# A transformer block with 32 ranked experts: the late tiles in another order, with their records, transposes and bias products

## The chip, the core and the metric

The kernel runs on one core of a Trainium2 chip. The metric is the device time of one execution in microseconds; before, the median of three runs is 299.98 us (299.43 to 300.33). The profile is one execution of its own, taken by the hardware profiler.

## What is computed

Cut to what matters; `x` has 1024 tokens of 512 numbers, everything is f32.

```python
x = x + ffn0(conv(x, cond_128, weight, c_weight, fside_S_0), w_gate, w_up, w_down)   # grouped conv of 9 taps; silu(gate) * up, down
y = mixed_1x1(x, cond_128, ...)                                                      # per-sample 32x32 kernel and bias
logits = y @ gate_w.T                                                                # 32 experts
w, idx = top_k(logits, 2); w = softmax(w)
combine = zeros((1024, 32)).at[arange(1024)[:, None], idx].add(w)
for e in range(32):
    acc = acc + combine[:, e:e+1] * (y @ expert_w[e].T + expert_b[e])
return x + acc
```

The kernel computes the two chosen experts of each token and no others: it sorts the 2048 pairs of token and expert by expert and multiplies tiles of rows.

## The kernel before

**Stages.** Up to some 125 us TensorE makes the tables of the first feed-forward layer and its first hidden half, and then the rest of that layer; up to about 183 us the last token tiles are routed. From 174 us on the expert stage runs, which is all that the change touches.

**Ranks.** The experts are ranked by how many tokens of the first half of the tokens chose them. Rank r's weights (512 x 512, 1 MB) are read from the place that `order` holds. Every rank has a fixed number of 32-row groups, by the plan at lines 83 to 136; what does not fit goes to a loop at the end that is skipped when nothing is left (line 1600 and below).

**Tiles.** A tile has 128 rows in groups of 32 or 64, each group of one rank: `pairs` gives tiles of two ranks with 64 rows each, `quads` four ranks with 32, `three_and_one` one rank with 96 and one with 32. `GROUPS_OF_TILES` (line 96) lists 21 tiles in the order in which they are worked on. Before it is:

| tiles | ranks |
|---|---|
| 0 to 3 | 0 and 4, 1 and 5, 2 and 6, 3 and 7 |
| 4 | 8, 9, 10, 11 |
| 5 to 8 | 0 and 4, 1 and 5, 2 and 6, 3 and 7 |
| 9 | 0, 1, 2, 3 |
| 10 | 10 and 11 |
| 11 to 14 | 8 and 24, 9 and 25, 12 and 26, 13 and 27 (three groups and one) |
| 15 to 19 | 14 and 19, 15 and 20, 16 and 21, 17 and 22, 18 and 23 |
| 20 | 28, 29, 30, 31 |

Tiles 0 to 4 (below `FIRST` = 5) hold tokens of the first half only. Tiles from 15 (`FIRST_B`) on are multiplied in two halves of 256 output columns, so that the left half of the output can be finished while the right one is computed (`STEPS`, line 133): the left halves of 15 to 19, the right ones of 15 to 17, the left half of 20, the right ones of 18, 19 and 20.

**What each tile does.** SyncE loads its records (`load_recs`, line 535: token, row and weight of each of the 128 rows; tiles of a group share a semaphore). GpSimd gathers the tokens' rows into `yg` (`gather_tile`, 665) and scatters finished rows to `r_tab` (`scatter_step`), one after the other on one queue. TensorE transposes yg (`transposes`, 1462, records at L1459), VectorE copies the result to `xT` (`xt_evac_tile`, 1046, records at L1044), TensorE multiplies with the weights (`product`, 1474, records at L1487; c0 and c1 bound the four chunks of 128 inner rows, two instructions for each group and chunk), and ScalarE evicts it with the row's weight (`evac`, L831). A product raises `r_mm` when it is done, a transposition `xt_mm`. The transposes of tile t+1 stand on TensorE ahead of the product of tile t, or in its middle.

**Weights.** Sixteen buffers of 1 MB hold 32 loads (`load_w`, 523, on SyncE's queue). Loads 0 to 15 fill them: ranks 0 to 11, then 24, 25, 12, 26. Loads 16 to 31 are ranks 13, 27, 14, 19, 15, 20, 16, 21, 17, 22, 18, 23, 28, 29, 30, 31. Each takes the buffer whose last product comes earliest (`SECOND`, 149), and SyncE waits for that product:

```python
                if i >= NA:
                    sp.wait_ge(w_in[b], 16)
                    sp.wait_ge(r_mm, released(b))
```

`released(b)` is one more than the last tile that uses the buffer. Before, loads 16, 17, 18 and 19 wait for products 5, 6, 7 and 8, loads 20 to 23 for product 9, 24 and 25 for 10, 26 and 27 for 11, 28 and 29 for 12, 30 and 31 for 13.

**Beside the tiles.** TensorE also makes the bias products (`bias`, 1429, L1435: the experts' biases by the combine weights, four PSUM banks for each half of the tokens), VectorE adds them (`add_bias`, L1013), and TensorE and VectorE count what is left for the loop at the end (`hist` at L1443, L1591, L1597; VectorE L1148 to L1196).

**The end.** When all left halves are scattered, SyncE reads `r_tab` back (`load_parts`, 591) into weight buffers, VectorE sums (L1211, L1212), and the left half of the output is stored; then the same for the right.

Of the kernel before, what the change touches and what calls it, by code (L numbers as in the profile page):

```python
# [42 lines left out]
P = 128  # L43
# [16 lines left out]
DC = D // P  # L60
# [17 lines left out]
NA, QUAD, PAIR = 16, P // 4, P // 2  # L78
SPLIT, SPLIT_QUAD, NQ = 8, 12, 4
WHOLE, THREE, TWO, ONE = 10, 14, 24, 32  # L80


def pairs(rank, pos, n):
    return [[(PAIR * q, PAIR, rank + i + n * q, pos) for q in range(2)] for i in range(n)]


def quads(rank, pos):
    return [[(QUAD * q, QUAD, rank + q, pos) for q in range(4)]]


def three_and_one(rank, pos, other):
    return [[(QUAD * q, QUAD, rank + i, pos + QUAD * q) for q in range(3)] + [(3 * QUAD, QUAD, other + i, 0)] for i in range(2)]
# [1 line left out]


GROUPS_OF_TILES = (pairs(0, 0, 4), quads(SPLIT, 0),
                   pairs(0, PAIR, 4), quads(0, P), pairs(WHOLE, QUAD, 1),
                   three_and_one(SPLIT, QUAD, TWO), three_and_one(SPLIT_QUAD, 0, TWO + 2),
                   pairs(THREE, 0, 5), quads(TWO + 4, 0))
TILES = [tile for group in GROUPS_OF_TILES for tile in group]  # L100
RECS = tuple(itertools.accumulate(len(group) for group in GROUPS_OF_TILES))
# [104 lines left out]
def build_adaln_ffn(nc, a):  # L206
    ctx = ExitStack()
    with ctx:
# [297 lines left out]
        def _(sp):  # L506
# [54 lines left out]
                store_y(j)  # L561

            sp.wait_ge(recs_out, 2 * NT * 16)
            for g in range(2, 4):
                load_recs(g)
            for r in range(13, NA):
                load_w(r)
            for g in range(4, len(RECS)):
                load_recs(g)
            for r in range(NA, E):  # L570
                load_w(r)
# [284 lines left out]
        def _(dve):  # L856
# [189 lines left out]
            def xt_evac_tile(t):  # L1046

                last = [STEP[s_] + 1 for s_ in STEPS if s_[0] < t and x_slot(s_[0]) == x_slot(t)]
                xt_evac(t, x_slot(t), xt_bank(t), max(last, default=None))
# [86 lines left out]
            for t in range(2, FIRST):  # L1136
                xt_evac_tile(t)
            xt_evac_tile(FIRST)
            xt_evac_tile(FIRST + 1)
            for j in range(TPH):  # L1140
                add_bias(j)
            xt_evac_tile(FIRST + 2)
            for j in range(TPH, NT):
                add_bias(j)
            xt_evac_tile(FIRST + 3)

            dve.wait_ge(cnt_mm, 1)
# [67 lines left out]
        def _(pe):  # L1215
# [353 lines left out]
            product(3, 0, 2)  # L1569
            transposes(4)  # L1570
            product(3, 2, DC)
            product(4, 0, DC - 1)
            transposes(FIRST)
            product(4, DC - 1, DC)
            pe.wait_ge(eb_in, 16)
            pe.wait_ge(combt_done, 2)
            bias(0)
            transposes(FIRST + 1)
            product(FIRST, 0, DC)
            bias(1)  # L1580
            transposes(FIRST + 2)
            product(FIRST + 1, 0, DC)
# [155 lines left out]
```

## Time and profile before

| | us |
|---|---|
| median of three runs (lowest, highest) | 299.98 (299.43, 300.33) |
| the profiled execution | 301.31 |
| its span, first to last instruction | 299.4 |
| TensorE matmul busy | 264.8 (88%) |
| VectorE, ScalarE, GpSimd busy | 130.7, 77.3, 76.9 |
| mean granted TensorE clock | 0.962 |
| DMA, 58.13 MB | mean 194 GB/s |
| share of the chain that ended last: TensorE, DMA, issue | 66%, 19%, 6% |

The page's shares are means over stages with different limits; the change touches the stage from about 187 us on, so it is read by stretches and by the chain of waits. In the rows below PE is TensorE's matmuls, SPq SyncE's queue, L12 line 12 of the kernel. Square brackets behind a row of a timeline give the idle time of the engine just before it and what ended it. An f32 matmul is two instructions in the records, so a tile of two ranks has 16 and one of four groups 32. "remote" is a release that the profile could not place.

### The profile page before, as it was taken

What the parts mean: (1) busy time and instruction counts of PE and PEld (TensorE: products, weight loads), DVE (VectorE), ACT (ScalarE), POOL (GpSimd) and SP (SyncE); (2) the same over time, 40 slices, a digit from 0 to 9 for tenths busy, and PEclk for the clock granted to TensorE, in tenths of its full rate; (3) what the DMA queues carried; (4) which work ended last, traced back from release to release, by engine and by line L of the source; (5) the groups of instructions that cost most, each with busy time, mean ns of one, the idle gap of its engine ahead of it and who ended that gap; (6) DMA issues with size and microseconds to landing.
All of it is one profiled execution on the core that took longest, in us unless ns stands there. A gap on an engine that the chain in (4) does not pass through costs nothing.

```text
span 299.4 us, 4645 instructions
## 1 busy us (share of the span) xinstructions
PE 264.8 (88%) x1672; PEld 165.2 (55%) x1672; DVE 130.7 (44%) x386; ACT 77.3 (26%) x142; POOL 76.9 (26%) x77
## 2 busy tenths in 40 slices
PE   8878999999999999999999999989989999949100
PEld 3345677688777878788877743323324336625000
DVE  3358766767423424574414554117522412100535
ACT  1556664243111142333211122010011112111000
POOL 0523400000000000046142234542755543332300
PEclk9999999999999999999999999999999999997755
DMA  7990000000001000090099993596869999950977
GB/s 276 386 327 1 3 0 1 2 2 0 0 35 37 36 35 2 15 402 5 1 323 418 416 421 130 181 371 224 294 244 389 414 416 421 414 231 16 361 251 261
DMA packets 21671, 58.13 MB, mean 194 GB/s; under 512 B 4569, under 2 KB 12417, under 8 KB 17296
## 3 DMA queue, kind: packets, MB, share of 16 engines
q1 hardware_dynamic: 16304, 47.89, 42.0%
q0 software_dynamic: 3968, 8.43, 7.6%
q10 hardware_dynamic: 1376, 1.51, 1.5%
q8 instruction: 14, 0.23, 0.3%
q14 instruction: 9, 0.07, 0.1%
HBM read 50.70 MB, written 10.32 MB: 204 GB/s over the span
## 4 chain that ended last, share of the span: by engine, by line
PE 66%; DMA 19%; issue 6%; DVE 3%; SPq 2%; ACT 2%; POOLq 0%; ACTq 0%
PE bank L1341 26%; PE bank L1523 14%; PE bank L1487 11%; DMA wbuf<-in_w 8%; DMA wbuf<-r_tab 5%; PE bank L1396 3%; DMA yg<-y_tab,recs 3%; DMA xp_first<-in_xp 2%; PE bank L1224 2%; PE bank L1459 2%; PE bank L1417 2%; PE bank L1403 1%; PE bank L1286 1%; SPq L594 1%; DVE y0lo L902 1%
## 5 line engine op out<-in xcount | busy, mean ns | idle before, releaser
L1487 PE MATMUL bank<-wbuf,xT 128*32 128x512 f32 (+3 forms) x560 | 80.2, 522 | 6.2 <-DMA wbuf<-in_w 4.8
L1487 PEld LDWEIGHTS bank<-wbuf,xT 128*64 128x64 f32 (+1 forms) x560 | 29.8, 126 | 40.8 <-issue 34.2
L1523 PE MATMUL bank<-md,hid 128*128 128x512 f32 x176 | 48.2, 414 | 0.0
L627 POOL DMA_INDIRECT slots<-kept,sid x16 | 15.9, 996 | 122.3 <-DVE sid L1008 119.3
L831 ACT ACTIVATE res<-bank,recs 128x512 f32<-128x512 f32 (+1 forms) x27 | 15.9, 592 | 81.7 <-PE bank L1487 68.7
L1523 PEld LDWEIGHTS bank<-md,hid 128*128 128x128 f32 x176 | 31.7, 189 | 8.3 <-issue 2.9
L1341 PE MATMUL bank<-y0hi,mg 128*128 128x512 f32 x88 | 35.2, 411 | 0.6 <-ACT y0hi L713 0.6
L1044 DVE COPY xT<-bank 128x512 f32<-128x512 f32 x21 | 14.4, 691 | 46.7 <-PE bank L1459 45.1
L1341 PE MATMUL bank<-y0hi,mu 128*128 128x512 f32 x88 | 33.7, 396 | 0.7 <-DVE mu L906 0.7
L1341 PE MATMUL bank<-y0lo,mg 128*128 128x512 f32 x88 | 33.7, 394 | 0.2 <-DVE y0lo L902 0.2
L1341 PE MATMUL bank<-y0lo,mu 128*128 128x512 f32 x88 | 33.6, 393 | 0.0
L963 DVE TENSOR_TENSOR htmp<-bank,stmp 128x512 f32<-128x512 f32 x22 | 15.2, 691 | 30.7 <-PE bank L1341 18.6
L635 POOL DMA_INDIRECT yg<-y_tab,recs x21 | 21.4, 1021 | 25.1 <-DMA recs<-slots 10.3
L759 ACT ACTIVATE hid<-htmp 128x512 fp32r<-128x512 f32 x22 | 13.9, 630 | 23.8 <-DVE htmp L963 21.6
L643 POOL DMA_INDIRECT r_tab<-res,recs x15 | 15.3, 1020 | 15.9 <-ACT res L831 13.1
L1341 PEld LDWEIGHTS bank<-y0hi,mg 128*128 128x128 f32 x88 | 16.5, 188 | 5.2 <-issue 1.9
L755 ACT ACTIVATE stmp<-bank,small 128x512 f32<-128x512 f32 x22 | 15.2, 690 | 16.0 <-PE bank L1341 15.6
L1341 PEld LDWEIGHTS bank<-y0hi,mu 128*128 128x128 f32 x88 | 16.4, 188 | 4.7 <-ACT mu L728 1.1
L1341 PEld LDWEIGHTS bank<-y0lo,mg 128*128 128x128 f32 x88 | 16.4, 188 | 3.9 <-DVE y0lo L902 0.6
L1341 PEld LDWEIGHTS bank<-y0lo,mu 128*128 128x128 f32 x88 | 16.4, 188 | 3.3
L1459 PEld LDWEIGHTS bank<-cf,yg 128*128 128x128 f32 x84 | 8.9, 140 | 16.1 <-issue 15.2
L1211 DVE TENSOR_TENSOR acc<-acc,wbuf 128x512 f32<-128x512 f32 x8 | 5.5, 692 | 27.8 <-DMA wbuf<-r_tab 27.8
(187 smaller groups left out, 276.0 us busy)
## 6 DMA issues: line engine op xcount, KB each, us to landing
wbuf<-in_w SPq DMA_DIRECT2D x32, 1024.0 KB
wbuf<-r_tab SPq DMA_DIRECT2D x8, 512.0 KB, 6.0
acc<-in_x SPq DMA_DIRECT2D x1, 2048.0 KB, 15.1
y_tab<-yv SPq DMA_DIRECT2D x8, 256.0 KB, 4.2
base<-in_base SPq DMA_DIRECT2D x3, 352.0 KB, 7.3
xp_first<-in_xp SPq DMA_DIRECT2D x1, 1040.0 KB, 7.2
xp_second<-in_xp SPq DMA_DIRECT2D x1, 1040.0 KB, 9.4
out<-acc SPq DMA_DIRECT2D x4, 256.0 KB, 3.4
```

What stands on the lines that cost most here:

```text
L627: pool.indirect_dma_start(out=slots, out_offset=bass.IndirectOffsetOnAxis(ap=sid[:, j, k:k + 1], axis=0), in_=rec[:, j, k], in_offset=None ...
L635: pool.indirect_dma_start(out=yg[b][:], out_offset=None, in_=y_tab[0:HALF] if first else y_tab, in_offset=bass.IndirectOffsetOnAxis(ap=rec ...
L643: pool.indirect_dma_start(out=r_tab, out_offset=bass.IndirectOffsetOnAxis(ap=recs[:, slot, 1:2].bitcast(U32), axis=0), in_=res[b][:], in_o ...
L755: nc.scalar.activation(stmp[:, n % 2], G[n % 2][:], ACT.Silu, scale=wsc[:, 0:1]).then_inc(silu_done, 1)
L759: nc.scalar.activation(hid[:, :, 0, n % HC], tiles_of(htmp[:, n % 2]), ACT.Copy).then_inc(hhi_done, 1)
L831: nc.scalar.activation(res[b][:, columns(h)], in_place(bank_, h), ACT.Copy, scale=recs[:, slot, 2:3].bitcast(F32)).then_inc(res_done, 1)
L963: nc.vector.tensor_tensor(htmp[:, n % 2], UU[n % 2][:], stmp[:, n % 2], ALU.mult).then_inc(h_done, 1)
L1044: nc.vector.tensor_copy(xT[half_][:].rearrange("p c t -> p (c t)"), bank_[:]).then_inc(xt_done, 1)
L1341: v = mm(bank_[:], tab[:, r, n % HC], (y0hi, y0lo)[part][:, r, HALF * half:HALF * (half + 1)], start=(r == 0 and part == 0), stop=(r == R ...
L1459: v = nc.tensor.transpose(bank_[:, P * c:P * (c + 1)], yg[b][:, P * c:P * (c + 1)], ident)
L1487: v = mm(in_place(RS[n % 2], h)[p0:p0 + w], xT[x_slot(t)][:, c, p0:p0 + w], wbuf[buffer(r)][:, c, columns(h)], start=(c == 0), stop=(c == ...
L1523: v = mm(DN[j % 2][:], hid[:, t, part, c], md[:, c], start=(c == 0 and part == 0), stop=(c == HC - 1 and part == 1))
```

## The change

The diff, whole:

```diff
@@ -94,8 +94,8 @@
 
 
 GROUPS_OF_TILES = (pairs(0, 0, 4), quads(SPLIT, 0),
-                   pairs(0, PAIR, 4), quads(0, P), pairs(WHOLE, QUAD, 1),
-                   three_and_one(SPLIT, QUAD, TWO), three_and_one(SPLIT_QUAD, 0, TWO + 2),
+                   pairs(WHOLE, QUAD, 1), three_and_one(SPLIT, QUAD, TWO), three_and_one(SPLIT_QUAD, 0, TWO + 2),
+                   quads(0, P), pairs(0, PAIR, 4),
                    pairs(THREE, 0, 5), quads(TWO + 4, 0))
 TILES = [tile for group in GROUPS_OF_TILES for tile in group]
 RECS = tuple(itertools.accumulate(len(group) for group in GROUPS_OF_TILES))
@@ -561,11 +561,11 @@
                 store_y(j)
 
             sp.wait_ge(recs_out, 2 * NT * 16)
-            for g in range(2, 4):
+            for g in range(2, 7):
                 load_recs(g)
             for r in range(13, NA):
                 load_w(r)
-            for g in range(4, len(RECS)):
+            for g in range(7, len(RECS)):
                 load_recs(g)
             for r in range(NA, E):
                 load_w(r)
@@ -1136,12 +1136,12 @@
             for t in range(2, FIRST):
                 xt_evac_tile(t)
             xt_evac_tile(FIRST)
-            xt_evac_tile(FIRST + 1)
             for j in range(TPH):
                 add_bias(j)
-            xt_evac_tile(FIRST + 2)
+            xt_evac_tile(FIRST + 1)
             for j in range(TPH, NT):
                 add_bias(j)
+            xt_evac_tile(FIRST + 2)
             xt_evac_tile(FIRST + 3)
 
             dve.wait_ge(cnt_mm, 1)
@@ -1569,14 +1569,14 @@
             product(3, 0, 2)
             transposes(4)
             product(3, 2, DC)
-            product(4, 0, DC - 1)
+            product(4, 0, DC)
             transposes(FIRST)
-            product(4, DC - 1, DC)
             pe.wait_ge(eb_in, 16)
             pe.wait_ge(combt_done, 2)
             bias(0)
+            product(FIRST, 0, 2)
             transposes(FIRST + 1)
-            product(FIRST, 0, DC)
+            product(FIRST, 2, DC)
             bias(1)
             transposes(FIRST + 2)
             product(FIRST + 1, 0, DC)
```

**Order of the tiles.** Tiles 0 to 4 and 15 to 20 stay. Now 5 is the tile of ranks 10 and 11, 6 to 9 are those of three groups and one (8 and 24, 9 and 25, 12 and 26, 13 and 27), 10 is ranks 0 to 3, and 11 to 14 are ranks 0 and 4, 1 and 5, 2 and 6, 3 and 7. The loads keep their order, since the ranks come into first use in the same order. Their buffers change: loads 16 and 17 now wait for product 5, 18 and 19 for 6, 20 and 21 for 7, 22 and 23 for 8, 24 and 25 for 11, 26 and 27 for 12, 28 and 29 for 13, 30 and 31 for 14.

**Records.** All record loads of tiles 5 to 14 now stand ahead of weight load 13 on SyncE's queue. Before and now, behind the last store of y (y_tab); recs are the records, wbuf_116 is buffer 13:

```order
L543 DMA y_tab<-yv 128x512
L539 DMA recs<-slots 64x16 x2
L539 DMA recs<-slots 32x4 x4
L527 TENSOR_LOAD order
L527 ISA x2
L533 ISA
L533 DMA wbuf_116<-in_w 128x2048
```

```order
L543 DMA y_tab<-yv 128x512
L539 DMA recs<-slots 64x4 x2
L539 DMA recs<-slots 96x8
L539 DMA recs<-slots 32x8
L539 DMA recs<-slots 96x8
L539 DMA recs<-slots 32x8
L539 DMA recs<-slots 32x4 x4
L539 DMA recs<-slots 64x16 x2
L527 TENSOR_LOAD order
L527 ISA x2
L533 ISA
L533 DMA wbuf_116<-in_w 128x2048
```

Six record loads more, those of the tiles of three groups and one and of ranks 10 and 11 with those of ranks 0 to 7, come ahead of the weights; the six for tiles 15 to 20 stay behind weight load 15.

**Transposes and bias products on TensorE.** Before and now, from the last quarter of product 4 on (wbuf_91, 112, 113, 114 are buffers 8 to 11, wbuf_83 and 87 are buffers 0 and 4; yg_120, 121 and 122 are the gathered rows of tiles 5, 6 and 7):

```order
L1459 MATMUL bank<-cf,yg_120 128x128 x4
L1487 MATMUL bank<-wbuf_91,xT_96 32x512
L1487 MATMUL bank<-wbuf_112,xT_96 32x512
L1487 MATMUL bank<-wbuf_113,xT_96 32x512
L1487 MATMUL bank<-wbuf_114,xT_96 32x512
L1435 MATMUL bank<-eb,combT 128x512 x4
L1459 MATMUL bank<-cf,yg_121 128x128 x4
L1487 MATMUL bank<-wbuf_83,xT_97 64x512
L1487 MATMUL bank<-wbuf_87,xT_97 64x512
```

```order
L1487 MATMUL bank<-wbuf_91,xT_96 32x512
L1487 MATMUL bank<-wbuf_112,xT_96 32x512
L1487 MATMUL bank<-wbuf_113,xT_96 32x512
L1487 MATMUL bank<-wbuf_114,xT_96 32x512
L1459 MATMUL bank<-cf,yg_120 128x128 x4
L1435 MATMUL bank<-eb,combT 128x512 x4
L1487 MATMUL bank<-wbuf_113,xT_97 64x512
L1487 MATMUL bank<-wbuf_114,xT_97 64x512
L1487 MATMUL bank<-wbuf_113,xT_97 64x512
L1487 MATMUL bank<-wbuf_114,xT_97 64x512
L1459 MATMUL bank<-cf,yg_121 128x128 x4
```

The last quarter of product 4 moved ahead of the transposes of tile 5, and the transposes of tile 6 moved from ahead of product 5 into its middle, behind the first bias product.

**VectorE.** The bias sums and the copies of xT swap places in the same way:

```order
 L1044 COPY xT_96<-bank 128x512
 L1044 COPY xT_97<-bank 128x512
-L1044 COPY xT_96<-bank 128x512
 L1013 TENSOR_TENSOR acc<-acc,bank 128x512 x4
-L1044 COPY xT_97<-bank 128x512
+L1044 COPY xT_96<-bank 128x512
 L1013 TENSOR_TENSOR acc<-acc,bank 128x512 x4
+L1044 COPY xT_97<-bank 128x512
 L1044 COPY xT_96<-bank 128x512
```

The first four bias sums now come ahead of the copy for tile 6, the other four ahead of that for tile 7. ScalarE's and GpSimd's orders are the same as before.

## Rows read from the trace of the kernel before

**Rows 1.** The page, part 2: what DMA moved in 40 slices, GB/s.

```profile
GB/s 276 386 327 1 3 0 1 2 2 0 0 35 37 36 35 2 15 402 5 1 323 418 416 421 130 181 371 224 294 244 389 414 416 421 414 231 16 361 251 261
```

**Rows 2.** Timeline of TensorE (PE), 174 to 200 us; columns: start us, us, engine, line.

```profile
192.52 4.65 PE L1487 MATMUL bank<-wbuf,xT 128*64 128x512 f32 x32
198.51 0.63 PE L1459 MATMUL bank<-cf,yg 128*128 128x128 f32 x4 [1.35 <-DMA yg<-y_tab,recs]
```

**Rows 3.** The same, 200 to 300 us.

```profile
206.38 0.66 PE L1459 MATMUL bank<-cf,yg 128*128 128x128 f32 x4
...
211.44 3.65 PE L1487 MATMUL bank<-wbuf,xT 128*64 128x512 f32 x16
...
221.41 3.64 PE L1487 MATMUL bank<-wbuf,xT 128*32 128x512 f32 x32 [1.42 <-DVE xT L1044]
...
230.09 3.92 PE L1487 MATMUL bank<-wbuf,xT 128*32 128x512 f32 x32
...
257.44 7.13 PE L1487 MATMUL bank<-wbuf,xT 128*64 128x256 f32 x64 [0.50 <-DMA wbuf<-in_w]
268.82 9.04 PE L1487 MATMUL bank<-wbuf,xT 128*32 128x256 f32 x96 [4.26 <-DMA wbuf<-in_w]
```

**Rows 4.** The chain of waits that ended last; columns: start us, us, who.

```profile
190.69 7.68 DMA yg<-y_tab,recs
...
243.71 24.98 DMA wbuf<-in_w
...
268.82 2.73 PE bank L1487 x32
...
272.92 2.35 DMA r_tab<-res,row_halves
```

**Rows 5.** Timelines of SyncE's DMA issues (SPq), in several stretches.

```profile
186.97 3.15 SPq L539 DMA_DIRECT2D recs<-slots  x6
190.89 2.62 SPq L533 DMA_DIRECT2D wbuf<-in_w  x3
...
205.61 5.59 SPq L533 DMA_DIRECT2D wbuf<-in_w  x2
...
220.74 10.91 SPq L533 DMA_DIRECT2D wbuf<-in_w  x6
...
286.85 2.17 SPq L594 DMA_DIRECT2D wbuf<-r_tab  x4
```

**Rows 6.** Stretches: us, busy PE, PEld, DVE, ACT, POOL; clock, DMA share, GB/s.

```profile
205.00:225.00 20.00, 18.58 (x117) 6.70 (x115) 8.91 (x35) 2.64 (x4) 11.47 (x12) 1.00 0.72 259
...
233.40:262.00 28.60, 28.10 (x240) 14.08 (x237) 6.49 (x10) 5.60 (x10) 12.35 (x13) 1.00 1.01 416
...
269.80:273.20 3.40, 3.40 (x28) 1.59 (x21) 0.00 (x0) 0.47 (x1) 0.28 (x1) 0.51 0.00 0
```

**Rows 7.** Timeline of ScalarE (ACT), 172 to 300 us: evictions of products.

```profile
220.63 1.27 ACT L831 ACTIVATE res<-bank,recs 128x512 f32<-128x512 f32 x2 [9.21 <-PE bank L1487]
225.82 0.69 ACT L831 ACTIVATE res<-bank,recs 128x512 f32<-128x512 f32 x1 [3.93 <-PE bank L1487]
```

**Rows 8.** Timeline of GpSimd (POOL), 140 to 300 us.

```profile
207.57 1.02 POOL L635 DMA_INDIRECT yg<-y_tab,recs  x1 [9.26 <-PE bank L1459]
...
279.30 1.45 POOL L654 DMA_INDIRECT r_tab<-res,row_halves  x1 [0.93 <-ACT res L831]
```

**Rows 9.** Timeline of VectorE (DVE), 172 to 300 us.

```profile
199.89 0.69 DVE L1044 COPY xT<-bank 128x512 f32<-128x512 f32 x1 [6.57 <-PE bank L1459]
...
207.07 0.69 DVE L1044 COPY xT<-bank 128x512 f32<-128x512 f32 x1 [2.17 <-PE bank L1459]
207.68 2.47 DVE L1013 TENSOR_TENSOR acc<-acc,bank 128x512 f32<-128x512 f32 x4
```

**Rows 10.** Waits, 190 to 300 us: us in total, times, longest.

```profile
DVE lst L1182 <- remote: 3.7, 1, 3.7
...
DVE junk L1148 <- remote: 1.4, 1, 1.4
```

## The prediction

> **What bounds the kernel now.** I read the page's row of DMA rates by slice first (a slice is 7.5 us): from slice 20 on, at 150 us, the experts' weights flow at about 420 GB/s, then for six slices at half of it, then again at about 415 up to 262 us [rows 1]. So I looked at whether TensorE has idle time in the expert stage that hangs on these transfers. There are four gaps [rows 2, 3]: 1.35 us at 198.5 (the gathered tokens of tile 5 not there), 1.42 us at 221.4 (the copy of xT for tile 9), 0.50 us at 257.4 and 4.26 us at 268.8, the last two ended by weight loads. Between the gaps TensorE goes from one instruction to the next: a tile costs 3.65 us of product and about 0.6 of transposes, a half product 1.78 (four in 7.13).
>
> The chain of waits runs over the last gap [rows 4]: the last weight load is issued at 243.7, lands 25.0 us later, and from there one path leads to the end: half product, eviction, scatter, read-back of the left half, sums, read-back of the right half, sums. What ends the kernel is thus the landing of weight load 31 plus 30.7 us.
>
> Why is that load late? Because the DMA engines stood half empty earlier. The SP rows show loads 13 to 15 at 190.9, and of the sixteen that follow two from 205.6 on and the next only from 220.7 [rows 5]; each waits until its buffer's last product is done. DMA moved 259 GB/s from 205 to 225 and 416 from 233.4 to 262 [rows 6]. Fourteen of the sixteen, 14 MB for which the engines had room from 205 on, were started at 220 to 244.
>
> **The change, part by part.**
>
> *Order of tiles, and with it the buffers.* Loads 0 to 15 are the same and go to the same buffers. Before, products 5 to 8 release one buffer each and product 9 four. Now product 5 (ranks 10, 11) releases two, 6, 7 and 8 two each, 9 and 10 none, and 11 to 14 two each. Eight of the sixteen late loads are thus free by the end of product 8 (four before). The rest is TensorE work in another order: a tile of four 32-column groups takes 3.64 us and one of two 64-column groups 3.65 [rows 3], so nothing.
>
> When does load 31 land? All times here are those of before less 1.4 (next part). Loads 16 and 17 go at about 204, 18 and 19 a tile later, 20 to 23 behind products 7 and 8, at the latest from 219.2 if those products are reported as late as now; they are through by 235. Loads 24 and 25 wait for product 11: it ended at 234.0 before [rows 3], and the report of a product comes up to 0.8 later (product 9 ends at 225.05 and is evicted at 225.82 [rows 3, 7]), so 233.3 now. A load on its own: 1.05 MB at 416 GB/s is 2.5 us, plus about 2.3 that even a small transfer takes from issue to landing (the scatter of 2.35 [rows 4]), so 4.8, at 238.1. In a full queue, while each 4.2 us a tile is gathered and one scattered (0.52 MB, 125 GB/s), 291 GB/s are left, 3.6 us a load: three loads, 248.9. Later, with half scatters, the gap rows give the pace: the loads awaited at 257.4 and 268.8 are four apart, 2.84 us each, so load 31 at 260.3. TensorE wants it at 268.8 - 4.3 - 0.5 - 1.4 = 262.7. With 3.6 for all seven it would be 263.3. I take 260.3: both late gaps go, **0.50 + 4.26 us**. Bounds: 4.2 of the 4.8 (3.6 a load), all of it (2.84). Product 19 has loads 26 and 27, there by 245.3, ten us ahead.
>
> *What the gap also costs.* Left half of tile 20 took 2.73 us [rows 4], a half product otherwise 1.78. The granted clock was 0.51 from 269.8 to 273.2, with no DMA running: the 1.2 GHz level, entered after the 4.26 us of idleness; before, 1.00 [rows 6]. Without the gap TensorE goes on at 2.4 GHz: **0.95 us**. The two right halves after it lie beside the left half's read-back and cost nothing: the last right scatter is issued at 279.3 and, at 2.35 us, long landed when SP issues the second read-back at 286.9 [rows 5, 8].
>
> *Transposes and bias products.* Product 4's last quarter (8 instructions, 0.93 us) now stands ahead of the transposes of tile 5, which so start at 197.17 + 0.93 = 198.1. Their gather was issued at 190.7 and took 7.68 us beside three weight loads [rows 4]; now those come 3.1 us later (next part), so the gather has the engines to itself and takes between 2.35 (a scatter with idle DMA [rows 4]) and 7.68: nearer the first. The gap of **1.35 us** goes. New is that between these transposes and product 5 only a bias product stands (1.07): DVE starts the copy 0.7 us after the transposes start when TensorE runs on (206.38 to 207.07 [rows 3, 9]), and takes 0.69, so 1.38, under 0.59 + 1.07: no wait. After an idle start (198.51 to 199.89) it was 1.38 + 0.69 = 2.07, which would cost 0.4. I take 1.4 for the place, bounds 0.9 and 1.5. The swap on DVE (bias sums and xT copies) is covered: bias sums of 2.47 us end a microsecond or more before product 6 and 7 want their xT.
>
> *Record loads moved ahead.* Six more record DMAs, 0.53 us of SP time each (3.15 for six [rows 5]), go ahead of load 13, which is issued at 194 and not 190.9, with the same for 14 and 15. Tile 7 wants load 13 at about 210, so ten us of cover. In return the gather of tile 10 no longer waits until 207.6 [rows 8]; nothing waited for it, so zero.
>
> *Left as it is.* The 1.42 us at 221.4. It hangs on a late report: product 7 ends at 215.1 by its instructions, but ACT evicts it only at 220.6, together with product 8, and DVE copies xT for tile 9 at the same time (TensorE resumes at 221.4, when that copy is done) [rows 3, 7].
>
> **Sum:** 4.26 + 0.50 + 0.95 + 1.35 = 7.06 us. The profiled execution took 301.3 (span 299.4), the median is 299.98; so 292.9 us by the median.
>
> **The rivals.**
>
> *The late report goes too: 291.5.* The narrow matmuls of the histogram and the list come ahead of a tile with 64-column groups now, and there DVE waits 1.4 and 3.7 us for their reports [rows 10]; where a tile with 32-column groups follows (product 9, behind L1591) it is evicted at 225.8, 0.8 after its end [rows 7]. After the change both are followed by 32-column tiles. Then product 9 starts 1.42 us earlier and all behind it. Against: it is a pattern of three cases without a mechanism. The Trainium skill (TensorE: Matmul & The Clock Gate, The cost: per-tile semaphore tail) gives tens of ns from a last matmul to its semaphore increment; the trace shows microseconds at this place, so the rule speaks for this rival only if the lateness is accidental.
>
> *Load 31 still ends last: 295.5.* Each pair of loads behind products 11 to 14 starts into a shorter queue than now. If the first three after load 24 take the 4.8 us of a load alone and the last four 3.2 (between 2.84 and 3.6), load 31 lands at 238.1 + 14.4 + 12.8 = 265.3, a gap of 2.6 us stays, and the time is 295.5. For it speaks that the margin is only 2.4 us. The Trainium skill (DMA: Bandwidth & Descriptors, the paragraph on three numbers under Where 436 GB/s comes from) says that HBM at about 358 GB/s per core binds such loads; by that estimate the loads would take 4.5 and then 3.3 us, load 31 would land at 264.8, and the time would be 295.0. The trace measured 416 over 28.6 us [rows 6] and does not agree, so that figure adds nothing to this rival's chance. Against the rival: loads 24 and 25 find 20 to 23 barely through, and TensorE's pace releases a pair every 4.2 us, less than two loads take.
>
> *Slower: 303.* The last two loads now wait for product 14 (245.1) and the pairs before for 11, 12, 13. If loads behind product 11 came to run one at a time at their 4.8 us, load 31 would land at 238.1 + 7 x 4.8 = 271.7, 3.0 later than now. It decides from 4.5 us a load. Against: at 245 four loads are still queued, so the queue has no reason to run dry.
>
> *No change.* TensorE finds another wait of 7 us, such as tile 9's load 17, now issued only behind product 5. It lands by 212 and is wanted at 220.
>
> **Chances.** Forecast 0.50, late report gone 0.22, load 31 last 0.19, no change 0.03, slower 0.04 and unnamed slower 0.02. A measurement of this kernel can tell 0.3% (0.9 us) from no change. Faster 0.91, same 0.03, slower 0.06. The range runs from 291.0, half a us under the first rival, to 296.4, the end of the second with the clock loss added.
>
> **What would show it.** Right: no idle time at the product of the left half of tile 20; clock 1.00 to the end of the products; SP issuing eight late loads by about 223; the transposes of tile 5 near 198.1 with no wait; the chain of waits running over TensorE and no longer over a 25 us weight load. Wrong: a wait on weights ahead of a half product, a gap of TensorE over 0.5 us ahead of product 5, or a weight load in the chain.

## The result, and the profile after

| | before | after |
|---|---|---|
| median, us (lowest, highest) | 300.0 (299.43, 300.33), 4 runs | 296.79 (295.39, 297.97), 4 runs |
| ratio, 95% interval | | 0.9883 (0.9857 to 0.9908) |
| the profiled execution, us | 301.31 | 297.97 |
| its span, us | 299.4 | 296.1 |
| mean granted TensorE clock | 0.962 | 0.956 |
| TensorE busy, share of the span | 88% | 90% |

The change makes the kernel 3.2 us faster (1.1% by the medians, 1.2% by the ratio). I forecast 292.9 us, so 7.1 us faster, with a range of 291.0 to 296.4; the measured median lies 0.4 us above the range. The sign was right and less than half of the gain came. The profiled execution is the slowest of the four (297.97 us), and its mean clock is the lowest: 0.956, where the others have 0.963, 0.963 and 0.969.

The stage's early gaps are gone. TensorE's timeline of the changed kernel, which answers to [rows 2, 3]:

```profile
192.37 5.51 PE L1487 MATMUL bank<-wbuf,xT 128*64 128x512 f32 x40
197.81 0.66 PE L1459 MATMUL bank<-cf,yg 128*128 128x128 f32 x4
198.40 1.14 PE L1435 MATMUL bank<-eb,combT 32*128 32x512 f32 x8
...
218.49 3.64 PE L1487 MATMUL bank<-wbuf,xT 128*32 128x512 f32 x32 [0.18 <-ACT res L831]
...
253.69 7.13 PE L1487 MATMUL bank<-wbuf,xT 128*64 128x256 f32 x64
264.36 10.11 PE L1487 MATMUL bank<-wbuf,xT 128*32 128x256 f32 x96 [3.54 <-DMA wbuf<-in_w]
```

The transposes of tile 5 follow product 4 without a wait (before, 1.35 us), the four half products ahead of tile 20's start without one (0.50), and the 1.42 us at the late report are gone. The 0.18 us in their place are another wait. The profile names ScalarE's eviction, but of the things that this product (tile 9) waits for in the code, load 17 is the one that came last: it landed at 218.35, 0.14 us ahead of the product, and load 31 is ahead of its product by the same 0.14 (264.22 and 264.36). But the big one stayed: 3.54 us ahead of the left half of tile 20, where 4.26 stood. The chain of waits still runs over a weight load, and the left half product behind it is slower than before (3.68 us, 2.73 in [rows 4]):

```profile
244.66 19.56 DMA wbuf<-in_w
264.36 3.68 PE bank L1487 x32
269.41 2.34 DMA r_tab<-res,row_halves
273.56 7.89 DMA wbuf<-r_tab
```

The sum over that chain: the left half of tile 20 starts 4.46 us earlier (268.82 to 264.36), of which four places make 1.35 + 0.50 + 1.24 (1.42 less the new 0.18) + 0.72 = 3.81; the rest lies in small differences of the instructions between. What follows takes 31.7 us instead of 30.6, mostly the half product at the lower clock (0.95). 4.46 - 1.16 = 3.3 us, the difference of the spans.

Why does load 31 land so late? SyncE's DMA issues after, against [rows 5]:

```profile
186.82 7.12 SPq L539 DMA_DIRECT2D recs<-slots  x12
194.72 2.59 SPq L533 DMA_DIRECT2D wbuf<-in_w  x3
197.35 4.11 SPq L539 DMA_DIRECT2D recs<-slots  x6
204.09 40.90 SPq L533 DMA_DIRECT2D wbuf<-in_w  x16
```

Loads 16 to 31 now go out one pair after another from 204.1 to 245.0, as the new buffer order was to bring. But load 13 starts at 194.7, 3.8 us later than before. The stretches (us, busy PE, PEld, DVE, ACT, POOL; clock, DMA share, GB/s), against [rows 6]:

```profile
194.00:204.00 10.00, 10.00 (x70) 3.27 (x72) 3.81 (x6) 1.41 (x3) 7.56 (x9) 1.00 0.89 319
204.00:231.00 27.00, 26.82 (x230) 9.45 (x227) 12.47 (x51) 4.16 (x7) 12.85 (x13) 1.00 1.02 411
231.00:246.00 15.00, 15.00 (x83) 5.94 (x82) 2.77 (x4) 2.77 (x5) 6.12 (x6) 1.00 1.01 408
246.00:259.00 13.00, 13.00 (x114) 8.14 (x114) 2.77 (x4) 2.75 (x6) 5.17 (x6) 1.00 0.94 390
259.00:264.30 5.30, 1.82 (x18) 0.93 (x14) 0.00 (x0) 0.95 (x2) 2.69 (x3) 0.89 0.35 136
264.30:275.00 10.70, 10.11 (x96) 5.17 (x96) 0.00 (x0) 1.83 (x4) 2.95 (x3) 0.73 0.19 58
```

The reader is to see two things. From 204 to 246 us the 16 DMA engines are busy without a break (share 1.01 to 1.02): loads 13 to 15 are not through when load 16 is issued, and it queues behind them. And from 259 to 264.3, while TensorE waits for load 31, only a third of the engines' time is used: half of the load's parts have landed by 259.5, and the rest dribble in.

The landing times below are read from the DMA records of the trace: a load raises its semaphore by 16, once for each of its parts, and it has landed with its last. There are 16 DMA engines too, so I take a part for the share of one engine; the records do not name it. In before, i, j and k some parts of some loads are missing from the records, in after, n, o, l and m all or nearly all are there. Under "spread" stands how long after the first part of load 31 its last one landed. All are us from the start of the span.

| | 16 issued | 16 | 23 | 24 issued | 24 | 31 | spread | gap at tile 20 | span |
|---|---|---|---|---|---|---|---|---|---|
| before | 205.6 | 210.6 | 244.1 | 232.8 | 247.9 | 268.7 | 6.3 | 4.26 | 299.4 |
| after | 204.1 | 214.9 | 238.8 | 231.0 | 242.4 | 264.2 | 8.7 | 3.54 | 296.1 |

My forecast had load 23 through by 235, load 24 issued at 233.3, alone, and landed at 238.1, and load 31 at 260.3. From load 24 to load 31 it took 21.8 us, against 22.2 forecast. So the pitch held and the starting point failed: load 24 was issued at 231.0, 2.3 us earlier than I had it, and still landed 4.3 us later, since the queue emptied itself of load 23 only at 238.8.

### The profile page after: what moved, and what is told of

It is laid out like the page before. It is cut to its first block, busy times and chain, and to the rows that moved or that the text cites. A ratio compares the mean times of both kernels' runs of the same rounds, so it can differ in the third digit from the quotient of the medians.

```text
span 296.1 us, 4645 instructions
## 1 busy us (share of the span) xinstructions
PE 265.4 (90%) x1672; PEld 164.2 (55%) x1672; DVE 130.6 (44%) x386; ACT 77.3 (26%) x142; POOL 76.8 (26%) x77
## 4 chain that ended last, share of the span: by engine, by line
PE 77%; DMA 14%; DVE 3%; ACT 2%; SPq 2%; issue 1%; ACTq 0%; POOLq 0%
PE bank L1341 27%; PE bank L1487 20%; PE bank L1523 14%; DMA wbuf<-in_w 7%; DMA wbuf<-r_tab 5%; PE bank L1459 3%; PE bank L1396 3%; DMA xp_first<-in_xp 2%; PE bank L1224 2%; PE bank L1417 2%; PE bank L1403 1%; PE bank L1286 1%; SPq L594 1%; DVE y0lo L902 1%; PE bank L1234 1%
## 5 line engine op out<-in xcount | busy, mean ns | idle before, releaser
L1487 PEld LDWEIGHTS bank<-wbuf,xT 128*64 128x64 f32 (+1 forms) x560 | 28.8, 129 | 40.8 <-issue 34.6
L1523 PEld LDWEIGHTS bank<-md,hid 128*128 128x128 f32 x176 | 31.7, 189 | 8.3 <-issue 2.9
L973 DVE SCALAR_TENSOR_TENSOR acc<-bank,small,acc 128x512 f32<-128x512 f32 x8 | 6.0, 751 | 26.3 <-PE bank L1523 26.3
```

Source lines behind the costliest of these rows:

```text
L1487: v = mm(in_place(RS[n % 2], h)[p0:p0 + w], xT[x_slot(t)][:, c, p0:p0 + w], wbuf[buffer(r)][:, c, columns(h)], start=(c == 0), stop=(c == ...
L1523: v = mm(DN[j % 2][:], hid[:, t, part, c], md[:, c], start=(c == 0 and part == 0), stop=(c == HC - 1 and part == 1))
```

## The experiments

Two explanations of the late load 31 stood against each other. **The queue:** from load 16 on the weights' queue never runs dry, and load 31 lands 15 loads behind load 16. **The release:** load 31 is late because products set its buffer free late, whatever was ahead of it. A second question came up in the first runs, the late reports. Ratios are to the kernel before, run on the same chip in the same session; its medians there were 301.39, 301.21 and 299.67 us.

### The parts of the change

**a_records_back.** The six moved record loads return behind weight loads 13 to 15.

```diff
-            for g in range(2, 7):
+            for g in range(2, 4):
                 load_recs(g)
             for r in range(13, NA):
                 load_w(r)
-            for g in range(7, len(RECS)):
+            for g in range(4, len(RECS)):
```

> The changed kernel with the record loads of tile 8 and of all later tiles again behind weight loads 13 to 15 on SyncE's queue, as before. Two theories of the gap of 3.54 us that is left ahead of the left half of tile 20 (load 31 lands at 264.4). QUEUE: from load 13 (issued at 194.7) to load 31 the weight queue never runs dry, so load 31 lands one queue length (19 loads at about 3.65 us) behind load 13, and the six record loads ahead of load 13 cost their 3.2 to 3.9 us once more at the end. Then load 13 goes at about 191, load 31 lands near 260.8, the gap is under 0.5 us, and the time falls from 296.8 to about 292.5 to 293.5. RELEASE: load 31 lands a fixed time after product 14 releases its buffer, then nothing changes: 296.8 +- 0.7. Under both, tile 8's records now land near 204, so its gather could open a gap of 0 to 1.5 us on TensorE near 209.

Measured: 301.54 us, ratio 1.0003 (0.998 to 1.0026). Load 13 is issued at 190.0 again and there is no gap at tile 20, but nothing is gained on before. TensorE loses 7.4 us inside product 7, which takes from 210.4 to 221.4 (11.0 us, otherwise 3.64) with idle pieces:

```profile
212.50 1.07 PE L1487 MATMUL bank<-wbuf,xT 128*32 128x512 f32 x4 [0.36 <-issue]
213.92 3.94 PE L1487 MATMUL bank<-wbuf,xT 128*32 128x512 f32 x13 [0.35 <-issue]
218.23 3.20 PE L1487 MATMUL bank<-wbuf,xT 128*32 128x512 f32 x9 [0.37 <-issue]
```

In the same time VectorE and ScalarE stand idle for 9.5 and 11.6 us until a "remote" release; ScalarE evicts product 6 at 216.9, though its instructions end at 209.7. I call this a late stretch. The run was to isolate the record loads and did not, since the stretch hides the rest.

**d_order_only.** Tiles and record loads as in the change, the late tiles' transposes, bias products and copies in their old places (TensorE's part of the edit; VectorE's copies and bias sums move back likewise).

```diff
-            product(4, 0, DC)
+            product(4, 0, DC - 1)
             transposes(FIRST)
+            product(4, DC - 1, DC)
...
-            product(FIRST, 0, 2)
             transposes(FIRST + 1)
-            product(FIRST, 2, DC)
+            product(FIRST, 0, DC)
```

> The changed kernel with the transposes, bias products and bias sums in the places they had before; order of tiles and of records as changed. If the sum of the prediction held (each gap of TensorE adds to the end) this is 1.35 us slower: 298.1. QUEUE: TensorE's gap ahead of tile 5 only eats into the time it spends waiting for load 31, and load 13 does not depend on it: within 0.5 us of 296.8, with the gap at tile 20 shorter by what the gap at tile 5 takes. It also tells whether the gather of tile 5, now with no weights beside it, is in time at 197.2 without the moved quarter of product 4.

Measured: 298.94 us, 0.9929 (0.9903 to 0.9955), with a late stretch ahead of product 5 (3.42 us at 204.0) and no gap at tile 20.

**b_loads_early.** Weight loads 13 to 15 go ahead of all record loads and of the wait for the records.

```diff
+            for r in range(13, NA):
+                load_w(r)
             sp.wait_ge(recs_out, 2 * NT * 16)
-            for g in range(2, 7):
-                load_recs(g)
-            for r in range(13, NA):
-                load_w(r)
-            for g in range(7, len(RECS)):
+            for g in range(2, len(RECS)):
                 load_recs(g)
```

> The changed kernel with weight loads 13 to 15 issued right behind the last store of y (about 178 us) and not behind the wait for the last records (186.8) and twelve record loads. QUEUE: the 3 MB flow while the DMA engines stand nearly idle (67 GB/s from 182 to 194), loads 16 on find an empty queue at 204, load 31 lands at about 204 + 5 + 15 x 3.4 = 260 or earlier, no gap is left, the clock stays at full speed to the end of the products, and the time is 291 to 292.5. RELEASE: no change, 296.8 +- 0.7. Risk under both: the last records' scatters and the record loads share the engines with 3 MB of weights, so the gather of tile 5 comes 0 to 2 us later; TensorE has 4 us of cover for it.

Measured: 298.79 us, 0.9899 (0.9864 to 0.9935). No gap at tile 20; a late stretch of 4.39 us ahead of product 5, and half the clock behind it from 202.9 to 209.7.

**c_half_loads.** Loads 16 to 19 fetch half of their weights; the other half is left out.

```diff
-                sp.dma_start(wbuf[b][:], a["w"][bass.ds(e, 1)].rearrange("a p c d -> p (a c) d")).then_inc(w_in[b], 16)
+                n = DC // 2 if 16 <= i < 20 else DC
+                sp.dma_start(wbuf[b][:, 0:n], a["w"][bass.ds(e, 1)].rearrange("a p c d -> p (a c) d")[:, 0:n]).then_inc(w_in[b], 16)
```

> The changed kernel with weight loads 16 to 19 fetching only the first two of four chunks (0.5 MB each; the products of tiles 9 and 15 then multiply part of the weights that were there before, so this part of the result is left out). Everything else, all waits too, stays. QUEUE: 2 MB less ahead of load 31 is about 7 us less, load 31 lands near 257, no gap, time 291 to 292.5. RELEASE: the last loads are issued as before and land as before, 296.8 +- 0.7.

Measured: 299.57 us, 0.993 (0.9904 to 0.9957), again with 4.40 us ahead of product 5 and no gap at tile 20. In all four the gap at tile 20 was gone, but so it would be by the late stretch alone, which delays TensorE and leaves the loads more time. These four tell nothing between queue and release. They tell that a second thing costs as much.

### The late stretch

**after_again.** The changed kernel itself, unedited, on another chip.

> The changed kernel itself again, on the chip of the other runs of this group. In the three variants that share its TensorE program (half loads, early loads, records back) TensorE's results are reported 2 to 9 us late in one stretch (tile 5 in two, tile 7 in one) and the time lost there hides what the loads give; in the profile of the changed kernel they were reported in time. CHANCE (the late stretch comes and goes between executions or chips): here the changed kernel may show it too, with a gap of 4 to 5 us ahead of product 5 and a time of about 298 to 299, and otherwise 296 to 297 with the gap at tile 20. LOADS (the variants' load order brings it on): 296 to 297.5, reports in time as before.

Measured: 299.17 us, 0.9929 (0.99 to 0.9957), 2.4 us above the 296.79 of the first measurement, though before was only 1.2 us above its own. Its timeline of TensorE, then its waits of VectorE and ScalarE (us in total, times, longest):

```profile
204.01 3.68 PE L1487 MATMUL bank<-wbuf,xT 128*64 128x512 f32 x8 [4.45 <-DVE xT L1044]
```

```profile
DVE xT L1044 <- remote: 10.1, 1, 10.1
ACT res L831 <- remote: 8.1, 1, 8.1
```

So the stretch is not made by the edits: of two profiled executions of the changed kernel one has it and one has not. They ran on different chips, so whether the chip or the execution decides is not shown. VectorE copies xT at 203.3 though the transposes of tile 5 ended at 198.5 by their records, 4.8 us before, and TensorE waits for the copy. (The profile models the ends of matmuls, so it cannot tell a late report from a TensorE that is itself late.) In the profiles of before, a, b, c, d and this one the late reports lie inside a run of GpSimd's indirect DMAs that follow each other at 0.3 us. The run of this execution, and the first step behind it (GpSimd's timeline from the second step on; six steps of the run are left out):

```profile
191.58 1.01 POOL L635 DMA_INDIRECT yg<-y_tab,recs  x1 [0.30 <-issue]
...
200.80 1.02 POOL L635 DMA_INDIRECT yg<-y_tab,recs  x1 [0.31 <-issue]
204.78 1.02 POOL L643 DMA_INDIRECT r_tab<-res,recs  x1 [2.95 <-ACT res L831]
```

The copy comes 1.45 us after the run's last step ended at 201.8. That suggested spacing the gathers: from tile 5 on, each gather waits for the transposes of the tile four places ahead of it (the count of transposed tiles, xt_mm, has reached t - 3).

```diff
-                if t >= U:
-                    pool.wait_ge(xt_mm, t - U + 1)
+                if t >= FIRST:
+                    pool.wait_ge(xt_mm, t - 3)
```

**k_before_spaced.** This edit on the kernel before.

> The kernel before with only the spacing of the gathers. Its profile has two late stretches, 211 to 220.5 and 226 to 231, both inside runs of GpSimd's DMAs. BURST: both go; product 7 is evicted at about 215.2 and not 220.6, the gap of 1.42 us at 221.4 goes, weight loads 18 and 19 start 5 us earlier, and with them those behind: load 31 lands 1 to 3 us earlier, 297.5 to 299.5 where the kernel before has 300 to 301.4. OTHER: both stretches stay and the time is that of before within 0.5 us.

Measured: 301.09 us, 1.0002 (0.9973 to 1.003). The stretches at 211 to 220 and 226 to 231 are gone (one of 3.3 us is left), tile 9 has no gap, and the time is unchanged. Load 31 lands at 267.4, 1.3 us earlier than in the profile of before, but TensorE now waits longer for it (5.63 us) and the 96 matmuls behind take 10.01 us instead of 9.04, at the lower clock:

```profile
254.77 7.13 PE L1487 MATMUL bank<-wbuf,xT 128*64 128x256 f32 x64 [0.46 <-DMA wbuf<-in_w]
267.53 10.01 PE L1487 MATMUL bank<-wbuf,xT 128*32 128x256 f32 x96 [5.63 <-DMA wbuf<-in_w]
```

**j_after_spaced.** The same edit on the changed kernel.

> The changed kernel with only the spacing of GpSimd's gathers as in the other. BURST: no late report in any run; the gathers that ran beside loads 13 to 15 come later, the traffic is the same, so load 31 still lands near 264 and the gap of about 3.5 us at tile 20 stays: 295.5 to 297. OTHER: as the changed kernel on this chip.

Measured: 297.88 us, 0.9847 (0.9782 to 0.9912). No "remote" release is left in the stage, and the gap at tile 20 is back:

```profile
264.17 10.15 PE L1487 MATMUL bank<-wbuf,xT 128*32 128x256 f32 x96 [4.04 <-DMA wbuf<-in_w]
```

This is close to the profile of the first measurement (264.36, 3.54), now made by an edit. It gave what the first four lacked: a version of the change in which load 31 can be studied without the stretch.

**i_early_spaced.** b with spaced gathers.

> The early loads again, and GpSimd's gathers of tiles 5 to 20 each wait until the tile four before it is transposed (it was eight), so that GpSimd no longer issues eight to twelve indirect DMAs back to back from 190 to 208 us but about one gather and one scatter for each tile. BURST: in all traces the stretch of late reports lies inside such a run of GpSimd's DMAs and ends 1.1 to 1.4 us after its last one, so the run holds TensorE's reports up. Then no late report, no gap ahead of product 5, no gap at tile 20: 291.5 to 293.5. OTHER (the reports are late for a cause of their own, and GpSimd's run only ends there because it waits for them too): the late stretch stays, 298 to 299.

Measured: 295.49 us, 0.9791 (0.9739 to 0.9842), faster than both kernels. Load 31 lands at 263.5 and the x96 start at 263.79 behind 0.84 us of waiting, at full clock; the profile puts the end of this wait down to an eviction. It loses 0.60 us at 198.8, since the records and so tile 5's gather come later, and 1.34 at 201.8 behind a late copy of xT: it starts 2.3 us after the transposes start, where 1.4 was usual after an idle start (198.51 to 199.89 in [rows 2, 9]). It is a rest of the stretch.

### Queue or release

These four ran together on one chip, all with spaced gathers.

**l_two_early_spaced.** Loads 13 and 14 ahead of the records' wait, load 15 between the record loads.

```diff
+            for r in range(13, 15):
+                load_w(r)
             sp.wait_ge(recs_out, 2 * NT * 16)
-            for g in range(2, 7):
+            for g in range(2, 5):
                 load_recs(g)
-            for r in range(13, NA):
-                load_w(r)
-            for g in range(7, len(RECS)):
+            load_w(15)
+            for g in range(5, len(RECS)):
                 load_recs(g)
```

> The changed kernel with the gathers spaced by the TensorE's count, and with loads 13 and 14 of the weights issued ahead of the records' wait, load 15 between the record loads. Theory one (the queue: from load 16 on the weights' queue never runs dry, so that load 31 lands 15 loads behind load 16): load 16 finds a short queue and lands by about 209 to 210 instead of 212 to 214, load 31 by about 261, the gap ahead of the 96 matmuls at tile 20 is 0.9 us or less and the left half of tile 20 runs at full clock; span about 291 us, 8 us or more below the kernel before on the same chip. Theory two (the release: load 31 is set by when its buffer comes free, and not by the loads ahead of it): load 31 lands at 264 as in the version with spacing alone, with a gap of 3.5 to 4 us there; span 296.

Measured: 293.73 us, 0.9801 (0.9755 to 0.9847). Its chain of waits, its TensorE timeline, and its stretch before load 16:

```profile
244.55 16.93 DMA wbuf<-in_w
261.62 1.97 PE bank L1488 x32
```

```profile
261.62 7.40 PE L1488 MATMUL bank<-wbuf,xT 128*32 128x256 f32 x96 [0.91 <-DMA wbuf<-in_w]
```

```profile
196.00:204.00 8.00, 8.00 (x56) 2.60 (x48) 3.81 (x6) 0.69 (x1) 5.42 (x6) 1.00 0.69 233
```

Loads 13 and 14 are issued at 177.8 and 178.9, 17 us sooner than in j, and load 15 at 193.2, 3.6 sooner. Loads 16, 24 and 31 are issued within 0.6 us of where j issues them. What has moved are the transfers ahead of load 16, weights and, with the records, the first gathers. Load 16 finds engines with room (share 0.69, in j 0.97) and lands at 209.6 instead of 212.1, and load 31 lands at 261.5 instead of 264.0: 2.5 us at both ends of the queue. The gap falls to 0.91 us and the half product runs at full clock. The release theory expected no difference in the landing and falls.

**m_half_spaced.** j with the halved loads 16 to 19 of c.

> The changed kernel with the gathers spaced; loads 16 to 19 fetch only half of their weights (the other half is left out, about 7 us of transfer at the queue's full rate). The queue theory: load 31 lands about 257, no gap ahead of the left half of tile 20, full clock there, span 5 to 6 us below the same version with whole loads, about 291. The release theory: load 31 still lands at 264 and the gap of 3.5 to 4 us stays; span 296.

Measured: 293.51 us, 0.9785 (0.9744 to 0.9825). Load 31 at 260.9 and not at 257, with a gap of 0.46 us. The direction is the queue's, the size is not. Load 23 lands at 231.0 and load 24 is issued at 230.8: the queue is as good as dry there for once, what was saved before that is lost, and from then on the pace of the transfers starts at a release. Load 24 lands 5.4 us after its issue, at 236.2, and load 31 24.7 us later. So there are two limits, and the queue's is the later by 3.1 us in j. This is also the case that my forecast took for the change: 238.1 and 260.3.

**o_records_back_spaced.** j with the record loads of a.

> The changed kernel with the gathers spaced and the six moved record loads put back behind weight loads 13 to 15. The queue theory: load 13 is issued at about 190.9 instead of 194.7, load 31 lands about 260.5, the gap at tile 20 is about 0.5 us at full clock, span about 292 to 293, unless tile 8's gather, whose records then land at about 204, opens a gap of 1 to 2 us of its own. The release theory: load 31 at 264, gap 3.5 to 4 us, span 296.

Measured: 296.37 us, 0.9899 (0.987 to 0.9927). Load 13 is issued at 189.9 and load 16 lands at 210.0, 2.1 us earlier than in j, but load 31 lands at 264.3. A gap of its own has come, as the expectation allowed:

```profile
203.97 1.00 POOL L635 DMA_INDIRECT yg<-y_tab,recs  x1 [9.92 <-DMA recs<-slots]
```

```profile
211.09 0.63 PE L1459 MATMUL bank<-cf,yg 128*128 128x128 f32 x4 [1.77 <-DMA yg<-y_tab,recs]
264.45 7.40 PE L1487 MATMUL bank<-wbuf,xT 128*32 128x256 f32 x96 [1.83 <-DMA wbuf<-in_w]
```

In the new order of tiles the gather that waits until 204 for its records is one that TensorE soon wants (tile 8), and 1.77 us of idleness there, with 0.24 at tile 5, put the later releases back: load 24 is issued at 232.8 and load 31 at 246.5, 2.5 us later than in j. What the queue gained at its head the releases took back at its end, so this run agrees with neither theory's number. With the old order nothing waited for it. So moving the record loads ahead pays for the new order and takes its price from the weights, and neither is zero.

**n_order_spaced.** j with the old places of transposes and bias products, as in d.

> The changed kernel with the gathers spaced, but the late tiles' transposes, bias products and bias sums in their places of before: the gaps at tile 5 (1.35 us) and ahead of tile 19 (0.5 us) may come back. If what load 31 still costs absorbs them (the queue theory), the time is that of the version with spacing alone within 0.7 us, and the gap at tile 20 is shorter by as much as the gaps ahead of it are longer. If the terms add up as my prediction had them, the time is 1.4 to 1.9 us longer than that version's.

Measured: 297.77 us, 0.9923 (0.9894 to 0.9952); profiled span 295.8 against 296.0 for j. No gap came back at tile 5 or ahead of the four half products, and load 31 lands at 264.2, with 4.01 us of waiting:

```profile
198.27 1.14 PE L1435 MATMUL bank<-eb,combT 32*128 32x512 f32 x8
...
264.31 8.99 PE L1487 MATMUL bank<-wbuf,xT 128*32 128x256 f32 x96 [4.01 <-DMA wbuf<-in_w]
```

The queue theory's time holds. The reason I had given for it, that a longer gap early would shorten the one at tile 20, was not put to the test, since there was no early gap. What it does tell is that the swap of transposes and bias products is worth nothing once the record loads stand ahead of the weights: tile 5's gather then has the engines to itself, and that was enough to remove the 1.35 us. In n it lands at 195.0 and in after at 195.2, in before at 198.4; d, without spacing, has no gap there either. With the record loads behind the weights again and the swap in place 0.24 us (o) and 0.57 (a) are left.

The landings of this series beside those of after, in the same columns as above:

| | 16 issued | 16 | 23 | 24 issued | 24 | 31 | spread | gap at tile 20 | span |
|---|---|---|---|---|---|---|---|---|---|
| j | 203.6 | 212.1 | 237.5 | 230.3 | 240.3 | 264.0 | 8.7 | 4.04 | 296.0 |
| n | 203.8 | 212.4 | 237.6 | 230.5 | 240.4 | 264.2 | 8.4 | 4.01 | 295.8 |
| o | 204.3 | 210.0 | 235.7 | 232.8 | 240.6 | 264.3 | 6.2 | 1.83 | 294.1 |
| l | 204.2 | 209.6 | 234.6 | 230.9 | 238.3 | 261.5 | 5.3 | 0.91 | 291.5 |
| m | 204.1 | 209.0 | 231.0 | 230.8 | 236.2 | 260.9 | 4.8 | 0.46 | 291.2 |

The single parts tell more than the last one. First and last part to land, in us:

| | load 16 | load 24 | load 31 | first part of 31 after its issue |
|---|---|---|---|---|
| n | 209.5, 212.4 | 235.5, 240.4 | 255.8, 264.2 | 11.6 |
| o | 208.8, 210.0 | 237.5, 240.6 | 258.1, 264.3 | 11.6 |
| l | 209.0, 209.6 | 235.6, 238.3 | 256.1, 261.5 | 11.6 |
| m | 207.6, 209.0 | 235.2, 236.2 | 256.1, 260.9 | 11.7 |

From n to l, on the same chip, the last part comes 2.8 us sooner at load 16 and 2.7 at load 31, while the first part of load 31 comes no sooner. In all four the first part of load 31 lands 11.6 or 11.7 us after the load's issue. So each theory holds for one end of a load: the first part follows the release, and the last part carries the backlog from the head of the queue. Since the product waits for the last part, the backlog is what the kernel pays.

## Why the prediction was right and wrong

**The step that failed** is the landing of load 31, in "When does load 31 land?": loads 20 to 23 "are through by 235", load 24 lands at 238.1. I started the weights' queue empty at load 16. I had moved load 13 to 194 myself, in a later paragraph, and had not carried it over: loads 13 to 15 and the gathers then fill the engines until load 16 comes. Load 16 landed at 214.9, load 23 at 238.8 (forecast: by 235), load 24 at 242.4 (238.1) and load 31 at 264.2 (260.3). Load 17, which the rival *No change* had landing by 212, landed at 218.35 and held tile 9's product for 0.18 us. TensorE wanted load 31 at 253.69 + 7.13 = 260.8, so 3.54 us of the 4.26 stayed. The forecast pace of seven loads (22.2 us; measured 21.8 in after, 23.2 to 24.7 in l, j and m) was not the error. Run l, which has the spaced gathers too, puts the queue's beginning where I had it, and finds load 24 at 238.3, load 31 at 261.5 and 293.7 us.

**Term by term,** against the profile of after:

| term of the sum | forecast | measured |
|---|---|---|
| gap ahead of tile 20 | 4.26 | 0.72 |
| gap at 257.4 | 0.50 | 0.50 |
| clock at the left half of tile 20 | 0.95 | -0.95 |
| gap at tile 5 | 1.35 | 1.35 |
| late report at 221.4, less the new wait for load 17 | 0 | 1.24, spent in the wait for load 31 |
| sum | 7.06 | 2.86, of 3.3 in the spans |

**"Record loads moved ahead … so zero"** failed in both directions. Tile 7 did have cover (load 13 landed at 201.7, its product started at 209.8), but the price was not paid at tile 7. It was paid by the queue, at load 31: l against n, on the same chip, has load 31 landed 2.7 us sooner and is, with the clock, 4.0 us faster. I looked for who waits for load 13, and not for what queues behind it. And the gain was not zero either: o shows 1.77 us at tile 8 when the record loads stay behind, and the 1.35 us that I booked under the transposes came from this move.

**The clock.** The mechanism was right and the sign of the term hung on the gap. The left half product took 3.68 us in after, all of it at the 1.2 GHz level, and 1.97 in l at 2.4 GHz: 1.71 us, where the gap of 4.26 us before had cost less, because the product's first us still ran at full clock (granted clock 1.00 from 268.8 to 269.8, 0.51 behind it). The 0.95 was itself too large: I took 1.78 us for the half product at full clock, which is a tile of two groups. This one has four groups and takes 1.97, so of the 2.73 us 0.76 was the clock. In these profiles the clock fell to the 1.2 GHz level during or just behind idle stretches of 3.4 to 5.6 us and did not behind those of 0.5 to 1.8.

**Tile 5 and VectorE.** The gap went, and the 0.4 us that I feared at product 5 did not come. The credit to the moved transposes was wrong (n and d have no gap without the move); what counted was the other half of my argument, the gather with the engines to itself: it took 4.8 us, landed at 195.2, and would have been in time for the old place at 197.2.

**The rivals.** *The late report goes too* came true as an event: the 1.42 us went, with 0.18 of waiting for load 17 in their place. The runs do not show that the change did it: the repeat of the same kernel has a late stretch elsewhere. And the pattern I gave for it, a narrow matmul ahead of a tile of 64-column groups, is not needed for it: b, c, d and the repeat of the change have the stretch at tiles 5 and 6, before any narrow matmul, and with GpSimd's DMAs spaced it is gone or short. The Trainium skill (TensorE: Matmul & The Clock Gate, The cost: per-tile semaphore tail) gives tens of ns for such a report. These traces do not agree: by the records of the matmuls VectorE starts 4.8 us behind the transposes in after_again, and ScalarE 7.1 us behind product 6 in a. *Load 31 still ends last* is what happened, with a landing at 264.2 (I had priced 265.3) and a gap of 3.54, and at 295.5 it was 1.3 us from the median. The mechanism I gave it, three loads after load 24 at 4.8 us each, was not it either: the loads behind 24 took 3.1 us each. The Trainium skill (DMA: Bandwidth & Descriptors, Where 436 GB/s comes from) had led to 295.0 by HBM at 358 GB/s; the stretch from 204 to 231 shows 411 GB/s, so the near hit is chance. *Slower* and *no change* did not come.

What stays open is how GpSimd's DMAs and the late reports hang together. Five of the six spaced versions of the change have no "remote" wait in this stage (j, l, m, n, o); of the seven profiles without spacing, six have at least one. But after had a run of such DMAs from 190.3 to 204.6, and o one from 204.0 to 215.6, without lateness. A run of them seems to favour it and is not enough. Nothing here shows the mechanism.

## What to carry to other kernels

When a transfer is moved back on a queue, ask not only when its own user wants it, but also whether the queue will still be empty when the next block begins: here a delay of 2.8 us in the last part of load 16 was still 2.7 us at the last part of load 31, fifteen loads on. Moving it pays if the head of the queue is filled earlier, and here two loads issued 17 us sooner and a third 3.6 us sooner were worth 4.0 us (l against n), more than the 3.2 of the whole change. And profile more than one execution before a gap is taken for the kernel's own: a stretch that was in one profile of the changed kernel and not in the other made four clean edits unreadable until it was removed. On one chip the kernel took 299.17 us as it is and 297.88 with the spaced gathers.

## What was not expected of the hardware

The parts of one load drift apart in a long full queue. The parts of load 31 landed within 4.8 us of each other in m, where the queue had been as good as dry once, and over 8.7 us in after and j, where it had been full since load 13. How long the queue has been full is not all of it: in k the parts of load 20 landed within 1.9 us and those of load 31, eleven loads later, over 9.4. In after the engines were busy for 0.35 of their time in the last 5.3 us before the load was complete. So in a full queue the mean rate (390 GB/s from 246 to 259) says when most bytes are through, and the slowest part says when the load has landed. In after that was several us later. Why some parts lag is not shown.
